# A Mamba scan plus expert FFN kernel: the sum over the states by transposes that accumulate in PSUM

## What is computed

```python
x  = einsum('ed,bld->bel', in_proj_w, hidden_states)       # 512 channels e, 512 positions l
xc = causal depthwise conv of 4 taps over l
u  = silu(xc + conv_b)
x_dbl = einsum('ke,bel->bkl', x_proj_w, u)                 # 16 rows dt_lo, 16 rows B, 16 rows C
delta = softplus(einsum('er,brl->bel', dt_proj_w, dt_lo) + dt_proj_b)
def step(state, xs):                                       # state: 512 channels x 16 states n
    dA = exp(d_t[..., None] * A)
    state = state * dA + (d_t * u_t)[..., None] * B_t[:, None, :]
    y_t = einsum('ben,bn->be', state, C_t)
y = (y + D * u) * silu(layernorm(x))                       # then x = x + y
```

## Time and profile before

| what | value |
|---|---|
| runs | 1376.32, 1381.13, 1383.25 us; median 1381.13 us |
| span of the profiled execution, first to last instruction | 1381.1 us |
| busy in the span | PE 1116.1 us (81%), DVE 868.8 (63%), POOL 606.3 (44%), ACT 520.5 (38%) |
| first scan of the first block starts | 56.96 us |
| last scan of the first block ends | 615.05 us |
| mean granted TensorE clock | 0.900 of full speed |

### The profile page before, as it was taken

How to read it: one execution, slowest core, us unless ns; L and a number is a source line. 1 busy time by engine, 2 the same in 40 slices (tenths; PEclk the granted TensorE clock), 3 DMA queues, 4 the chain that set the end, 5 groups by cost and what they waited for, 6 DMA issues and landing times.

```text
span 1381.1 us, 18552 instructions
## 1 busy us (share of the span) xinstructions
PE 1116.1 (81%) x4156; PEld 745.3 (54%) x4156; DVE 868.8 (63%) x745; ACT 520.5 (38%) x697; POOL 606.3 (44%) x424
## 2 busy tenths in 40 slices
PE   4657667677668756763499999999999999999994
PEld 2223222223223322323478888888888888888883
DVE  3799999999999999993732434343253434324321
ACT  3754456555654565222221323232231323213210
POOL 0398498668976798630201222222122222223211
PEclk8688888899778888895599999999999999999998
DMA  5333342336234524334521424242142433414210
GB/s 158 139 122 121 124 137 91 123 121 230 72 110 139 197 91 148 113 104 166 193 107 46 167 101 167 106 164 98 38 160 99 143 124 104 166 48 167 92 40 30
DMA packets 68892, 168.01 MB, mean 122 GB/s; under 512 B 9039, under 2 KB 11599, under 8 KB 68865
## 3 DMA queue, kind: packets, MB, share of 16 engines
q1 hardware_dynamic: 59824, 139.41, 29.4%
q0 software_dynamic: 9040, 28.32, 6.3%
HBM read 343.60 MB, written 18.35 MB: 262 GB/s over the span
## 4 chain that ended last, share of the span: by engine, by line
PE 49%; DVE 2%; DMA 1%; issue 0%; POOL 0%; ACT 0%; POOLq 0%; DVEq 0%
PE hp L1433 10%; PE hp L1432 10%; PE hp L1434 10%; PE yp L1432 5%; PE yp L1434 5%; PE yp L1433 5%; PE tp L1473 2%; PE xp L1426 1%; PE hp L1417 1%; PE yp L1481 0%; DMA work<-xln_dram,index 0%; DMA work<-out_dram,acc_index 0%; DMA out_dram<-work,out_index 0%; DVE R L1299 0%; POOL index L1045 0%
## 5 line engine op out<-in xcount | busy, mean ns | idle before, releaser
L293 POOL TENSOR_TENSOR ring<-du,bc 128x1024 f32<-128x1024 f32 x128 | 361.6, 2848 | 149.2 <-DMA bc<-bcs 80.9
L681 PE MATMUL yacc<-ring,ident 128*128 128x512 f32 x512 | 292.8, 711 | 139.0 <-DVE ring L544 138.2
L532 DVE TENSOR_TENSOR_SCAN ring<-dA,ring 128x1024 f32<-128x1024 f32 x128 | 290.9, 2275 | 6.8 <-ACT dA L356 3.5
L681 PEld LDWEIGHTS yacc<-ring,ident 128*128 128x128 f32 x512 | 106.4, 224 | 308.4 <-DVE ring L544 209.1
L356 ACT ACTIVATE dA<-delta,Acol 128x511 f32<-128x511 f32 (+1 forms) x256 | 165.7, 681 | 223.5 <-DVE ring L532 223.3
L1432 PE MATMUL hp<-w_hi,xT_hi 128*128 128x512 f32 x592 | 237.5, 401 | 0.9 <-DVE xT_lo L1329 0.9
L1433 PE MATMUL hp<-w_lo,xT_hi 128*128 128x512 f32 x592 | 236.6, 400 | 0.0
L1434 PE MATMUL hp<-w_hi,xT_lo 128*128 128x512 f32 x592 | 232.9, 393 | 0.0
L544 DVE TENSOR_TENSOR ring<-ring,bc 128x1024 f32<-128x1024 f32 x128 | 217.9, 1707 | 0.0
L1350 DVE TENSOR_TENSOR work<-hp,work 128x512 f32<-128x512 f32 x74 | 51.0, 690 | 232.3 <-PE hp L1434 194.4
L1069 POOL COPY out_index<-out_tab 128x1 uint32 x37 | 6.7, 181 | 356.4 <-DVE work L1336 356.4
(11 more groups left out here) (177 smaller groups left out, 1186.5 us busy)
## 6 DMA issues: line engine op xcount, KB each, us to landing
stage<-in_L_ffn_w_kernel_dram SPq DMA_DIRECT2D x160, 1024.0 KB
stage<-in_L_ffn_wo_kernel_dram SPq DMA_DIRECT2D x78, 1024.0 KB
bc<-bcs SPq DMA_DIRECT2D x128, 512.0 KB, 4.5
xall<-in_x_dram SPq DMA_DIRECT2D x1, 4096.0 KB, 15.1
xln_dram<-xlnb SPq DMA_DIRECT2D x4, 1024.0 KB, 7.8
out_dram<-xall SPq DMA_DIRECT2D x4, 1024.0 KB, 9.4
ctx_rows<-in_ctx_dram SPq DMA_DIRECT2D x4, 512.0 KB, 4.9
work<-xln_dram,index POOLq DMA_INDIRECT x39, 3.8
```

The costliest lines, as they stand in the source:

```text
L293: g_.tensor_tensor(ring[:, n % RING, :].rearrange("p (e l) -> p e l", e=2), cols(du, b, h * 2 * L, 2 * L).rearrange("p (e l) -> p e l", e= ...
L532: v_.tensor_tensor_scan(ring[:, n % RING, :], dA[n % 2][:, :, :].rearrange("p e l -> p (e l)"), ring[:, n % RING, :], 0.0, ALU.mult, ALU.a ...
L681: last = t_.matmul(yacc[:, e, :], ident[:, :], ring[:, n % RING, e * L:(e + 1) * L], start=False, stop=(n == UPH - 1))
```

## The change

The loops over the elements are written out (no loop on the engines any more), and the units' work is split otherwise. In a unit of the changed kernel:

- `du` is transposed once per half into `duT` (positions on partitions, 4 blocks of 128 positions x 256 channels), and `x_dbl` into `xdT`, so that B[n] is a column with one value per partition.
- The product with B is made in that layout, four *pieces* of 128 x 256 (`piece`): two on ScalarE (L159), one on POOL, one on VectorE (both L161).
- TensorE transposes the pieces back (`turn_in`, L674, eight transposes of 128 x 128) into one of two PSUM tiles `dB0`, `dB1`.
- VectorE scans (L516) with `dA` from SBUF (three tiles) and `dB` from PSUM, into one of six `ring` tiles.
- POOL multiplies by C (L265).
- TensorE adds to `yT` by eight transposes per unit with `is_transpose=True` that accumulate (`acc`, L691), so that `yT` has positions on partitions; the D term is eight matmuls of 128 x 128 (two instructions each).

So B isn't spread by DMA any more (64 loads of 512 KB stay, for C). The gate `zs` is transposed per element (`zs_T`, sixteen transposes and four copies), `g` isn't; `add_y` is one VectorE instruction. The Relu of softplus moves from ScalarE to VectorE (`relu`, L547), one subtraction falls away on POOL, and the reciprocal root starts from an integer guess on VectorE with three steps on POOL (14 small instructions instead of 6), without ScalarE. The statistics of all 16 blocks of `x` (L611) move from ahead of the first unit to its slot 4.

```diff
-RING = 8
+RING = 6
+DAS = 3
+BTS = 4
...
+        def piece(eng, engine, q, t, done, act=False):
...
+            o, i, s = dBT[:, q % BTS, t, :], duT[:, h, t, :], xdT[:, b % 2, t, 2 * DS + n:2 * DS + n + 1]
+            if act:
+                i = engine.activation(o, i, ACT.Identity, scale=s)
+            else:
+                i = engine.tensor_scalar(o, i, s, None, ALU.mult)
...
-                g_.tensor_tensor(ring[:, n % RING, :].rearrange("p (e l) -> p e l", e=2),
-                                 cols(du, b, h * 2 * L, 2 * L).rearrange("p (e l) -> p e l", e=2), B,
-                                 ALU.mult).then_inc(dbu_done, 1)
+            def times_c(q):
+                p = q // 2
+                pool.wait_ge(scan_done, q + 1)
+                if q % 2 == 0:
+                    pool.wait_ge(bc_in[p % 4], 16 * (p // 4 + 1))
...
+                g_.tensor_tensor(states, states, C, ALU.mult).then_inc(hc_done, 1)
...
-                v_.tensor_tensor_scan(ring[:, n % RING, :], dA[n % 2][:, :, :].rearrange("p e l -> p (e l)"), ring[:, n % RING, :],
+                dve.wait_ge(exp_done, q + 1)
+                dve.wait_ge(dB_full, q + 1)
+                if q >= RING:
+                    dve.wait_ge(acc_done, q - RING + 1)
+                v_.tensor_tensor_scan(ring[:, q % RING, :], dA[:, q % DAS, :, :].rearrange("p e l -> p (e l)"),
+                                      dB[q % 2][:, :, :].rearrange("p e l -> p (e l)"),
...
-                    last = t_.matmul(yacc[:, e, :], ident[:, :], ring[:, n % RING, e * L:(e + 1) * L], start=False, stop=(n == UPH - 1))
+            def turn_in(q):
+
+                for done in (bt_act, bt_pool, bt_dve):
+                    pe.wait_ge(done, q + 1)
+                if q >= 2:
+                    pe.wait_ge(scan_done, q - 1)
+                for e in range(2):
+                    for t in range(LB):
+                        last = t_.transpose(dB[q % 2][:, e, t * P:(t + 1) * P], dBT[:, q % BTS, t, e * P:(e + 1) * P], ident[:, :])
+                last.then_inc(dB_full, 1)
...
+                pe.wait_ge(hc_done, q + 1)
+                for t in range(LB):
+                    for e in range(2):
+                        last = t_.matmul(yT[:, t, e * P:(e + 1) * P], ring[:, q % RING, e * L + t * P:e * L + (t + 1) * P], ident[:, :],
+                                         start=False, stop=(n == UPH - 1), is_transpose=True, skip_group_check=True)
+                last.then_inc(acc_done, 1)
...
+                    if q + 2 < NU:
+                        turn_in(q + 2)
+                    if q >= LAG:
+                        acc(q - LAG)
```

More of the change, by code:

```diff
@@ L334, in _ @@
+            rstd_2(NB - 1)
         @block.scalar
@@ L511, in _ @@
-            turn(0, TURN0, 0, rest=False)
-            with act.Fori(1, NB - 1) as b:
-                turn(b, LOOP, b - 1)
-            turn(NB - 1, LAST, 0, nxt=False)
-            guess_2(NB - 1)
+                tap(0, eb)
+            silu_u(0)
+            x_dbl(0)
+            x_dbl_T(0)
+            dt_abs(0, 0)
+            soft(0, 0)
+            soft_log(0, 0)
+            du_T(0, 0)
+            act.wait_ge(consts_ok, 1)
+            act.wait_ge(zeros_ok, 1)
+            pieces(0)
+            pieces(1)
@@ L647, in _ @@
-            turn(0, TURN0, 0, rest=False)
-            with dve.Fori(1, NB - 1) as b:
-                turn(b, LOOP, b - 1)
-            turn(NB - 1, LAST, 0, nxt=False)
+                last.then_inc(dve_step, 1)
+                dve.wait_ge(dve_step, 4 + 4 * b + 2)
+                guess(rs2, mv2, 4 + 4 * b + 2, guess2)
+            for i in range(DAS):
+                last = v_.memset(dA[:, i, :, 0:1], 0.0)
+            last.then_inc(zeros_ok, 1)
+            conv(0, (0, 1))
+            conv(0, (2, 3))
@@ L694, in in_proj @@
-            def in_proj(uses, turn, eb):
-                if eb == 0:
-                    for i in range(KB):
-                        k = uses["T%d" % i]
-                        pe.wait_ge(freed[k % 2], before(k, turn) + 1)
-                k = uses["X%d" % eb]
-                use(k, turn)
-                for i in range(KB):
-                    last = t_.matmul(bank(k)[:, :], wT[:, i, eb * P:(eb + 1) * P], ctxT[:, i, :], start=(i == 0), stop=(i == KB - 1))
-                last.then_inc(filled[k % 2], 1)
@@ new lines, in ctx_T, with in_proj @@
+                    last.then_inc(done, 1)
+            def in_proj(b, ebs):
+                for i in range(KB):
+                    k = USE[f"T{i}.{b}"]
+                    pe.wait_ge(freed[k % 2], nth(k))
+                for eb in ebs:
+                    o, done = use(f"X{eb}.{b}")
+                    for i in range(KB):
+                        last = t_.matmul(o[:, :], wT[:, i, eb * P:(eb + 1) * P], ctxT[:, i, :], start=(i == 0), stop=(i == KB - 1))
+                    last.then_inc(done, 1)
@@ L750, in logits_of @@
                 for i in range(LB):
                     for d in range(DI // P):
-                        last = t_.matmul(bank(k)[:, i * 8:(i + 1) * 8], gT[:, i, d * P:(d + 1) * P], gate[:, d, :], start=(d == 0), stop=(d == DI // P - 1))
-                last.then_inc(filled[k % 2], 1)
-            def half(b, h, tasks):
-                for n in range(UPH):
-                    if n > 0:
-                        acc(b, h, n - 1)
-                    for f in tasks.get(n, []):
-                        f()
-                acc(b, h, UPH - 1)
@@ L787, in _ @@
+                        last = t_.matmul(o[:, i * 8:(i + 1) * 8], gT[:, i, d * P:(d + 1) * P], gate[:, d, :], start=(d == 0), stop=(d == DI // P - 1))
+                last.then_inc(done, 1)
             pe.wait_ge(ident_ok, 2)
@@ L801, in _ @@
+            o, done = use("DTT")
             for eb in range(EB):
-                last = t_.transpose(bank(k)[0:DR, eb * P:(eb + 1) * P], dt_rows[:, eb, :], ident[:, :])
-            last.then_inc(filled[k % 2], 1)
-            ctx_T(0, FIRST, 0)
-            for eb in range(EB):
-                in_proj(FIRST, 0, eb)
-            x_proj(0, FIRST, 0)
-            for eb in range(EB):
-                dt_proj(FIRST, 0, eb)
-            turn(0, TURN0, 0, rest=False)
-            with pe.Fori(1, NB - 1) as b:
-                turn(b, LOOP, b - 1)
```

955 lines of the change are left out of this document (520 added, 435 removed).

## The result

The changed kernel takes 1474.37 us (median of 4 runs, 1474.26 to 1474.81) against 1380.18 us of the kernel before on the same chip (4 runs, 1376.32 to 1383.25): a ratio of 1.068 with a 95% interval of 1.0655 to 1.0705. It is slower by about 94 us where 73 us less were forecast, and it lies outside the range.

The account below looks back on a forecast made before the run. VectorE was taken to bound the kernel before. After the change, VectorE and ACT with gaps, then POOL, bound each turn: 482 us of scans from 62.4 to 544.4 us; 1381.1 - 70.7 - 2 = 1308 us, range 1262 to 1348.

Parts of the forecast that it names:

- They do not fit without gaps: Slots 0 to 19 of a full turn: VectorE 75, ACT 75, POOL 68.5 us, plus 8 us of gaps, 83 us.
- the two units by which it can run ahead: Slots 0 to 19: ACT's 75 us of work is eased by a lead of two units.
- only two `dB` tiles in hand: Slots 6 and 9: input projection queued ahead of the next `turn_in`; VectorE's conv waits 1.5 us each.
- POOL's piece: New POOL instruction per unit: 0.45 us, between 0.29 and 0.58; above 0.6 us was a sign of being wrong.
- VectorE's piece: New VectorE instruction directly behind each scan: 0.25 us, between 0.185 and 0.30, plus 0.3 us waiting for POOL.
- the lost race: Rival: POOL's product starts first, VectorE's piece waits for all of it; 1516 us, chance 0.05; sign: median over 1 us.
- ACT's pieces: Two new ACT instructions of 256 columns per unit: 0.48 us each, 0.45 us in spacing.
- The clock: TensorE's granted clock through the scan: over 0.8 expected, 0.85 before; its work stays hidden above 0.64.
- The rival at half clock: TensorE's clock at 0.5 throughout the scan, 613 us of TensorE work; 1439 us, chance 0.04.
- The start and the tail: First scan starts near 62.4 us; the work behind the last scan gains 2 us.
- More gaps: Rival: piece waits 0.52 us, handovers cost twice, 4 + 8 us more in three turns; 1348 us, chance 0.17.

Follow-up runs that it names:

- experiment 1: Changed kernel with ACT's Exp issued two units ahead, before the slot's tasks: 1356.68 us, 0.9837 of the kernel before.
- experiment 4: Changed kernel with ACT's Exp issued one unit ahead of its tasks instead of none: 1390.54 us, 1.0066 of the kernel before.
- experiment 7: Changed kernel with Exp two units ahead and POOL's piece moved to ACT: 1343.15 us, 0.9724 of the kernel before.
- experiment 5: Changed kernel with POOL's piece moved to VectorE, which then makes two per unit: 1617.45 us, 1.1728 of the kernel before.
- experiment 3: Changed kernel with Exp two units ahead and TensorE's slot tasks issued ahead of `turn_in`: 1342.96 us, 0.9722 of the kernel before.
- Experiment 11: Kernel before with only the sum over states made by accumulating transposes, loops written out: 1349.7 us, 0.9787 of the kernel before; the experts' work differs.
- experiment 9: Changed kernel with Exp two units ahead, TensorE's tasks ahead of `turn_in`, and POOL's piece on ACT: 1337.19 us, 0.9669 of the kernel before.
- experiment 6: Changed kernel with POOL's piece moved to ACT, without Exp ahead: 1492.32 us, 1.0804 of the kernel before.
- experiment 12: Kernel before with only its loops over the elements written out on all engines: 1386.39 us, 1.0017 of the kernel before.

## Why the prediction was wrong, point by point

**What failed** is one step above all: "They do not fit without gaps", with its 8 us of gaps in slots 0 to 19. It rested on ACT having "the two units by which it can run ahead", and on counting only what a task costs beyond the tiles in hand. The working counts the free `dA` and `dBT` tiles, and doesn't ask whether ACT can reach its next Exp: its task waits for a TensorE result that waits for the scan of the same slot or of the one before. At such slots the lead in buffers was lost: at 230.35 us ACT was ahead of the scan, and at 247.33 us the scan waited for it. In the place of 8 us in each of three turns and 2 in the last, 26 us, stood 165.5 us, in 41 waits of 4.0 us on the mean, the longest 10.4 us. Experiments 1 and 4 show that it is this: nothing but the place of Exp in ACT's queue changed, and 84 and 118 us went. The prediction had even written that `turn_in` has "only two `dB` tiles in hand", and took it for VectorE's conv alone (1.5 us twice in each of three turns, 9 us; that wait, `DVE u L529 <- ACT u L330`, came to 20.7 us). ACT's load was not under-estimated: 406 us were forecast (128 x 2.19 + 126) and 382 measured.

By the sum: forecast were 128 x 2.70 + 85 = 431 us of VectorE's work and 51 us of idling in a stage of 482 us; measured are 454 and 192 us in 646. So 141 of the 163 us missed are idling, and 23 are work.

**POOL's piece** was put at 0.45 us between 0.29 and 0.58; it takes 957 ns at the median, 1066 on the mean, outside the bounds. The ceiling was wrong: a quarter of the two-input product of 1024 columns is no ceiling for a one-input product of 256. POOL's total came to 472 us instead of 431, and the sign that was named, a piece above 0.6 us, was met. This is a second error of the sum, hidden behind the first. In a stretch without tasks POOL sets the pace at 3.25 us a unit, where 2.98 was forecast:

```profile
237.05 2.34 POOL L265 TENSOR_TENSOR ring<-ring,bc 128x1024 f32<-128x1024 f32 x1
...
239.37 0.96 POOL L161 TENSOR_SCALAR dBT<-duT,xdT 128x256 f32<-128x256 f32 x1
...
240.30 2.33 POOL L265 TENSOR_TENSOR ring<-ring,bc 128x1024 f32<-128x1024 f32 x1
```

Over the stage POOL waited 171 us for scans, and moving its piece to ACT paid only once the circle was cut (about 14 us, experiment 7).

**VectorE's piece** takes 329 ns where 0.25 was said (bounds 0.185 to 0.30), again just outside. Its mean of 618 ns holds 0.29 us of waiting, where 0.3 was taken. That agreement is in part luck. The reason given, that the piece stands directly behind the scan and is issued first, holds where POOL has waited for the scan: in experiment 5 the first piece gets in, and the one behind it waits for a whole product. Where POOL is not idle, its product is still running when the scan ends, and the piece waits for the rest: 1.14 us at 235.15 and 238.40 us. The fewer pauses, the more often that happens: the median piece takes 708 ns in experiment 1 and 1060 ns in experiment 3, over the 1 us that the prediction had named as the sign of the lost race, and back at 328 ns in experiment 7, where POOL has no piece. The Trainium skill (SBUF — State Buffer, Who interferes with whom) says that who issues second blocks fully; the trace agrees, with 2.69 us for the pair.

**ACT's pieces** were put at 0.48 us, 0.45 in spacing: 496 ns each and 114.5/256 = 0.447 us. **TensorE**: eight transposes take 1.04 or 1.94 us, as said from the earlier trace rows.

**The clock**: 0.81 through the scan, where over 0.8 was said. The rival at half clock is out, though the granted clock is below the 0.85 of before. From 220 to 240 us TensorE has nothing but the transposes of `turn_in` and the sum. The clock was at 0.50 behind a pause of 5.3 us and rose to 1.00, where it stayed (columns as in the earlier trace rows):

```profile
222.00:224.00 2.00, 2.00 (x11) 2.00 (x10) 2.00 (x3) 2.00 (x5) 2.00 (x3) 0.50 0.00 0
226.00:228.00 2.00, 2.00 (x21) 2.00 (x20) 2.00 (x2) 2.00 (x5) 2.00 (x3) 1.00 0.17 70
238.00:240.00 2.00, 1.37 (x13) 1.41 (x14) 1.54 (x2) 0.00 (x0) 2.00 (x2) 1.00 0.00 0
```

So transposes alone were granted the full clock. The Trainium skill (TensorE: Matmul & The Clock Gate, Part 4: PE-mode transpose) says that the full clock doesn't engage in transpose mode, and the trace doesn't agree. Experiment 11 shows that transposes can still cost some of it, 0.65 on the mean in place of 0.85.

**The start and the tail**: first scan at 63.3 us, forecast 62.4; behind the last scan 1.6 us less than before, forecast 2.

**The rivals.** None was what happened. "More gaps" (1348 us) had in part the right kind of mechanism, handovers that come too late, but with 16 us of them in each of three turns, beside 4 us for the piece, where the waits for Exp alone came to 41; its size came from the same step. "VectorE's piece loses the race" gave a time on the right side, but not for the reason: in the changed kernel the median piece took 329 ns, where over 1 us was its sign. Of the signs that were named, VectorE at 80 to 90% (it was 70%), POOL near 90% (73%), the end of the scan near 545 us (709) and its length within 430 to 520 us (645) spoke against the forecast, and ACT was waited for at many slots: 71 of the 165.5 us lie at 12 to 19.

**And the idea**: with the two orders mended the change is worth 2.8% (experiment 3), and 3.3% with POOL's piece on ACT as well (experiment 9, 1337.19 us), 29 us short of the forecast 1308. Its stage of 507.8 us is 26 us above 482. VectorE still idles 61 us ahead of its scans there, 19.5 for `turn_in`, 12.1 for Exp and 28.4 with no wait that the profile shows; ACT, which now makes three pieces of four, is busy for 86%, but that this is the cause was not shown.

## What to carry to other kernels

Buffers in hand are not a lead. For every engine that feeds the bound, follow its queue back from the instruction that the bound needs: if a task ahead of it waits for another engine's result, and that engine's queue waits for the bound, the lead is lost at that slot, however many tiles are free. When such a chain is found, put the feeding instruction ahead of the tasks. Here two units were worth 118 us without an instruction more, and an edit tried before that (experiment 6) cost 18 us where it later gave 14.

## What the runs showed of the hardware

- A float32 TENSOR_SCALAR of 128 x 256 with a scalar per partition takes POOL 957 ns (912 at best), where its product of two tiles of 128 x 1024 takes 2369 ns: the smaller one costs 3.7 ns a column, the larger 2.3. VectorE does the same piece in 329 ns, ACT in 496.
- A VectorE piece directly behind the scan takes 0.33 us where POOL has waited for the scan, and 1.14 us where POOL's product is still running (at 235.15 us). A second piece, queued behind the first, waits for POOL's whole product: 2.69 us for the pair against 0.66 us. Moving 128 pieces of 0.33 us to VectorE made the kernel 143 us slower.
- Exchanging four matmul instructions of 512 columns for eight transposes of 128 lowered the granted clock of the scan from 0.85 to 0.65, with TensorE busy for 324 instead of 382 us (experiments 12 and 11). It cost nothing there, since VectorE was the bound. With sixteen transposes a unit it was 0.81, and 0.87 where the scan paused less (experiment 9). Between 226 and 240 us of the changed kernel, with nothing but transposes on TensorE, it was 1.00.
